# Attention with experts on one core: the first query job of a head behind the second score group, the last whole output tile behind the first group of last rows

## The chip, the core and the metric

The kernel runs on one core of one Trainium2 chip. The metric is the device time of one execution in microseconds (us), the median of several runs. A profile is one further execution, recorded instruction by instruction.

## The reference

Four sequences of 1024 tokens with 256 features are normalized, and from the normalized rows two things are made: a causal attention with 8 query heads of 128 that share one key and one value head, and a mixture of 8 experts of which each token uses two. The result is `x + attention * silu(experts)`.

```python
xn = _layernorm(x, axis=-1)
q = (xn @ Wq + bq)                  # 8 heads of 128
kv = xn @ Wkv + bkv                 # one key and one value head
q, k = q + pe, k + pe               # sinusoidal positions
scores = einsum('bhqd,bkd->bhqk', q, k) * scale
probs = softmax(where(causal, scores, finfo.min))
s = (probs @ v).reshape(B, T, 1024) @ Wo
g = silu(moe_top2(xn, router_w, router_b, w1, b1, w2, b2))
out = x + s * g
```

## The kernel before, in words

Three stages follow one another: `prologue` (normalize, route, split into halves), `experts`, and `attention` (L999 to L1520), which is the one that the change touches. Products are made in three passes of 16-bit halves (`PASSES`, L22): a value is kept as a high half and a low half, and high x high, high x low and low x high are added up.

**The attention stage.** There are 32 heads (4 sequences x 8 heads, `NH`), numbered n. The eight blocks of 128 query rows of a head are handled in five score groups i = 0 to 4, `GROUPS = ((7,), (6, 0), (5, 1), (4, 2), (3,))`: the block u needs u + 1 blocks of keys, so a group is 1024 columns of scores (the last one 512). A step is k = 5n + i. For every step, TensorE writes the scores of the group (`scores`, L1094); VectorE takes the row maxima (`maxima`, L1309); ScalarE the exponentials and their sums (`expo`, L1210); VectorE the reciprocals (L1340); ScalarE or GpSimd the high half of the probabilities (`high`, L1242 and L1435); VectorE, two steps later, the low half (`low`, L1345). The SP queue then issues transposes of the halves (`turn`, L1479), and in the following head TensorE multiplies them with the values, two blocks at a time in four value groups (`values`, L1124, in the order `PAIRS`). ScalarE and VectorE take high and low halves of that output (`o_high`, `o_low`).

**Jobs.** What a later head needs is projected in jobs, each into one PSUM bank of 128 x 512: two query jobs ("Q") per head, for the head after next, and in heads 4 to 7 of each of the first three sequences one key or value job ("K", "V") for the next sequence. Class `Jobs` (L290) lists them: `at` tells the step behind which a job is issued, `order` their order, `bank` the bank. Query jobs use bank "J" (`psJ`), key and value jobs bank "S" (`psS2`, the one of group 4's scores). A job is six matmuls of 512 columns (a value job 24 of 128) on TensorE (`project`, L1079), then VectorE adds the positions (`job_positions`, L1318; not for values), ScalarE takes the high half (`job_high`, L1229), VectorE the low half (`job_low`, L1326), which signals `jl_`. A job waits on `jl_` until the job before it in the same bank has been taken (`freed`, L1178-1179).

**Output tiles.** From head 9 on, TensorE also computes, at the end of each head, one whole tile of 128 output rows (`o_tile`, L1141, 24 matmuls of 256 columns) for the sequence before, into the same bank `psJ`. VectorE multiplies it by its gate at the start of the step after (`o_gated`, L1378, signals `ot_`), GpSimd adds the input rows, and the SP queue stores them. Because the bank is shared, the first query job of a head from 10 on waits for `ot_` (L1184-1185).

**The order around the change.** Every engine's order is written out by hand. TensorE's loop (L1170 to L1189) does for each head n and group i: the scores of the group; from i = 1 on value group i - 1 of the head before; the job of that step, if there is one; at i = 4, from head 9 on, an output tile. The first query job stands at i = 0, the key or value job at i = 1, the second query job at i = 2. ScalarE and VectorE take a job in the step after the one it was issued in. VectorE's order within a step is this (L1390 to L1405):

```python
if k - 1 in jobs.at:
    job_positions(jobs.at[k - 1])
if 1 <= k <= LAST:
    reciprocals(k - 1)
if k <= LAST and (k - 1) // 5 >= 1 and (k - 1) % 5:
    o_low((k - 1) // 5 - 1, (k - 1) % 5 - 1)
if k < LAST:
    maxima(k)
if k - 1 in jobs.at:
    job_low(jobs.at[k - 1])
if k >= 2:
    low(k - 2)
```

**The tail.** The last sequence's output is not done in tiles but as rows in four PSUM banks (`rows_out`, L1155), seven heads first and the eighth later. TensorE's tail (L1190 to L1206) is: the last whole output tile; a wait for the exponentials and for `al_`, the low output halves of head 30; last rows of pair 3 and of pair 0 for seven heads (42 matmuls each); then the value groups of head 31, in turn with the other rows.

Of the kernel before, what the change touches and what calls it, by code (L numbers as in the profile page):

```python
# [19 lines left out]
HEADS, HD = 8, 128  # L20
# [269 lines left out]
class Jobs:  # L290


    def __init__(self, heads):
        self.at, self.order, self.bank = {}, [], []
        for k in range(5 * heads):
            n, i = k // 5, k % 5
            b = n // HEADS
            job, bank = None, "J"
            if n == 0:
                job, bank = (("V", 0, 0), ("V", 0, 1), ("Q", 2, 0), ("Q", 2, 1), None)[i], ("J", "O0", "O1", "J", "")[i]  # L300
            elif i in (0, 2) and n + 2 < heads:
                job = ("Q", n + 2, i // 2)
            elif i == 1 and n % HEADS >= 4 and HEADS * (b + 1) < heads:
                job, bank = ("KKVV"[n % HEADS - 4], b + 1, n % 2), "S"
            if job:
                self.at[k] = len(self.order)
                self.order.append(job)
                self.bank.append(bank)

    def issued(self, k):  # L310

        return sum(1 for s in self.at if s < k)
# [686 lines left out]
def attention(nc, v):  # L999
# [6 lines left out]
    TILES = NT - QT  # L1006
    LAST = 5 * NH
    jobs = Jobs(NH)
# [3 lines left out]
    with ExitStack() as ctx:  # L1012
# [56 lines left out]
        def _(eng):  # L1069
# [24 lines left out]
            def scores(n, i):  # L1094

                k = 5 * n + i
# [10 lines left out]
                if i == 4 and k - 3 in jobs.at and jobs.bank[jobs.at[k - 3]] == "S":  # L1107
                    eng.wait_ge(jl_, jobs.at[k - 3] + 1)
# [15 lines left out]
            def values(n, s):  # L1124
# [14 lines left out]
                mm.then_inc(pv_, 1)  # L1139

# [29 lines left out]
            for n in range(NH):  # L1170
                for i in range(5):
                    k = 5 * n + i
                    scores(n, i)
                    if n and i:
                        values(n - 1, i - 1)
                    if k in jobs.at:
                        q = jobs.at[k]
                        if jobs.freed(q):  # L1178
                            eng.wait_ge(jl_, jobs.freed(q))
                        if jobs.bank[q] == "S":  # L1180
                            eng.wait_ge(ex_, 5 * n)
                        if n == 0:
                            eng.wait_ge(pl_, {"J": 4, "O0": 5, "O1": 6}[jobs.bank[q]])
                        if i == 0 and n >= HEADS + 2:  # L1184
                            eng.wait_ge(ot_, n - HEADS - 1)
                        project(*jobs.order[q], job_bank[jobs.bank[q]]).then_inc(jm_, 1)
                    if i == 4 and n > HEADS:
                        eng.wait_ge(jl_, jobs.issued(k + 1))
                        o_tile(n - HEADS - 1)  # L1189
            o_tile(TILES - 1)  # L1190
            eng.wait_ge(ex_, LAST - 1)
            eng.wait_ge(al_, 4 * (NH - 1))
            rows_out(3, 0, HEADS - 1)
            rows_out(0, 0, HEADS - 1)
# [14 lines left out]
        def _(eng):  # L1209
# [65 lines left out]
            for k in range(LAST + 2):  # L1275
                n, i = k // 5, k % 5
                if k - 1 in jobs.at:
                    job_high(jobs.at[k - 1])
# [19 lines left out]
        def _(eng):  # L1298
# [19 lines left out]
            def job_positions(q):  # L1318
                kind, m, j = jobs.order[q]
                if kind != "V":  # L1320
                    bank = job_bank[jobs.bank[q]]
                    eng.wait_ge(jm_, q + 1)
                    eng.scalar_tensor_tensor(bank, bank, SC / WS, pe_sb[:, j * 512:(j + 1) * 512],  # L1323
                                             ALU.mult, ALU.add).then_inc(jp_, 1)
# [65 lines left out]
            for k in range(LAST + 2):  # L1390
# [3 lines left out]
                if k - 1 in jobs.at:  # L1394
                    job_positions(jobs.at[k - 1])
# [6 lines left out]
                if k - 1 in jobs.at:  # L1402
                    job_low(jobs.at[k - 1])
# [144 lines left out]
```

## Time and profile before

| what | us |
|---|---|
| median of 3 runs | 1114.44 |
| the runs | 1115.57, 1114.44, 1110.93 |
| the profiled execution | 1122.9 |
| its span, first to last instruction | 1121.1 |
| mean granted clock of TensorE, of full speed | 0.989 |

The span holds 28441 instructions. The attention stage fills it from about 485 us on. Times in the rows further down are counted from the first instruction. In a timeline a row is one instruction, or several of one kind that follow one another (x6 are six): its start, its length, the engine, the line, what it writes and reads; in brackets the idle time ahead of it and who ended it. A matmul's end is a modelled one, and a following matmul normally starts before that end. The number of a head is worked out from the order of the query jobs.

### The profile page before, as it was taken

The numbers are of one execution on the slowest core, as the hardware profiler recorded it, in microseconds if no ns is written. First come the engines' busy times: TensorE is split into PE (matmuls) and PEld (weight loads), VectorE is DVE, ScalarE is ACT, GpSimd is POOL, SyncE is SP. The second block draws the span as 40 slices with busy tenths as digits, with TensorE's granted clock in tenths as the row PEclk, the third lists the DMA queues.
The fourth block names the chain that finished last, engine by engine and source line by source line (L and its number), as shares of the span: only waits on it lengthen the run. The fifth ranks groups of instructions, "written<-read, shape, count | busy, mean of one in ns | idle before, by whom it ended". The sixth has DMA issues, their size and how long they took to land.

```text
span 1121.1 us, 28441 instructions
## 1 busy us (share of the span) xinstructions
PE 1016.8 (91%) x10270; PEld 811.9 (72%) x10270; DVE 883.5 (79%) x1607; ACT 554.5 (49%) x1264; POOL 442.7 (39%) x499
## 2 busy tenths in 40 slices
PE   2536999999999999998989889999999999999997
PEld 1525888888888898755666667667777777777776
DVE  6894676676676454479999999998999999999972
ACT  3812223323323333346766666656666666666740
POOL 0013999899995100012323233333333333333331
PEclk9999999999999999998999999999999999999999
DMA  8547666756665512129987898988999888999993
GB/s 280 184 174 152 171 170 172 185 162 178 180 166 145 95 44 49 30 71 161 170 139 145 135 172 159 159 148 156 161 172 179 144 151 149 166 161 159 171 160 105
DMA packets 405896, 169.02 MB, mean 151 GB/s; under 512 B 348634, under 2 KB 396324, under 8 KB 405124
## 3 DMA queue, kind: packets, MB, share of 16 engines
q1 hardware_dynamic: 348704, 127.05, 57.0%
q10 hardware_dynamic: 50580, 22.45, 8.8%
q0 software_dynamic: 6480, 17.70, 7.4%
q8 instruction: 89, 1.46, 0.5%
q14 instruction: 43, 0.35, 0.1%
HBM read 51.66 MB, written 30.67 MB: 73 GB/s over the span
## 4 chain that ended last, share of the span: by engine, by line
DVE 27%; PE 20%; ACT 4%; issue 3%; DMA 2%; SPq 1%; ACTq 0%; DVEq 0%
DVE b_ph L1353 10%; DVE b_nmax L1314 8%; PE b_psO L1137 7%; PE b_psS L1118 5%; DVE b_outs L1361 2%; PE b_psJ L1075 2%; PE b_psJ L1151 2%; DVE b_psJ L1323 2%; ACT b_pr L1217 2%; PE b_psS L1162 2%; DMA b_pT<-b_ph 2%; ACT b_ph L1249 1%; PE b_psS L1075 1%; DVE b_Q L1337 1%; DVE b_f L1367 1%
## 5 line engine op out<-in xcount | busy, mean ns | idle before, releaser
L1442 POOL TENSOR_SCALAR b_ph<-b_pr,b_rrec 128x896 f16<-128x896 f32 (+4 forms) x160 | 109.3, 691 | 502.3 <-DVE b_rrec L1343 460.6
L938 ACT ACTIVATE h<-psU,bias 128x256 f32<-128x256 f32 (+1 forms) x320 | 125.1, 448 | 294.5 <-PE psU L858 170.4
L1217 ACT ACTIVATE b_pr<-b_psS,b_nmax 128x1024 f32<-128x1024 f32 (+7 forms) x256 | 187.3, 736 | 159.0 <-DVE b_nmax L1314 159.0
L1137 PE MATMUL b_psO<-b_pT,b_vp 128*128 128x128 f16 x3456 | 219.1, 221 | 20.5 <-DMA b_pT<-b_ph 20.4
L1137 PEld LDWEIGHTS b_psO<-b_pT,b_vp 128*128 128x128 f16 x3456 | 202.5, 99 | 29.6 <-issue 19.0
L858 PE MATMUL psU<-bxT,w_p 128*128 128x256 f16 (+1 forms) x1536 | 208.3, 273 | 16.5 <-DVE w_p L261 12.8
L1118 PE MATMUL b_psS<-b_kp,b_Q 128*128 128x512 f16 (+3 forms) x1152 | 220.2, 328 | 0.1
L1353 DVE SCALAR_TENSOR_TENSOR b_ph<-b_pr,b_rrec,b_ph 128x1024 f16<-128x1024 f32 (+7 forms) x256 | 209.9, 851 | 0.0
L871 PE MATMUL psY<-w_p,hp 128*128 x1512 | 206.4, 273 | 0.0
L959 DVE CAST hp<-h 128x512 f16<-128x512 f32 (+1 forms) x160 | 85.9, 537 | 137.1 <-ACT h L938 135.0
L1314 DVE TENSOR_REDUCE b_nmax<-b_psS 128x1 f32<-128x1024 f32 (+7 forms) x256 | 183.3, 748 | 8.6 <-PE b_psS L1121 8.6
L858 PEld LDWEIGHTS psU<-bxT,w_p 128*128 x1536 | 150.1, 99 | 35.6 <-issue 17.4
L1118 PEld LDWEIGHTS b_psS<-b_kp,b_Q 128*128 128x128 f16 x1152 | 103.6, 98 | 78.6 <-issue 2.3
L871 PEld LDWEIGHTS psY<-w_p,hp 128*128 128x128 f16 x1512 | 147.8, 98 | 17.4
L961 DVE TENSOR_TENSOR hp<-h,hp 128x512 f16<-128x512 f32 (+1 forms) x160 | 134.8, 843 | 5.5
L171 POOL DMA_INDIRECT rowx<-xn_split,who x71 | 80.4, 1132 | 106.7 <-DVE who L755 78.3
L1249 ACT ACTIVATE b_ph<-b_pr,b_rrec 128x1024 f16<-128x1024 f32 (+2 forms) x96 | 78.7, 853 | 0.5 <-DVE b_rrec L1343 0.5
L1451 POOL DMA_INDIRECT b_yg<-expert_outputs,pos x64 | 72.2, 1128 | 14.7 <-issue 14.1
L1361 DVE SCALAR_TENSOR_TENSOR b_outs<-b_psO,bias,b_outs 128x256 f16<-128x256 f32 x128 | 60.8, 475 | 19.0 <-ACT b_outs L1226 19.0
L1226 ACT ACTIVATE b_outs<-b_psO,bias 128x256 f16<-128x256 f32 x128 | 60.4, 472 | 19.0 <-PE b_psO L1137 19.0
L1151 PE MATMUL b_psJ<-b_wo,b_outs 128*128 128x256 f16 x576 | 66.8, 273 | 2.1 <-DVE b_G L1382 2.1
L250 POOL TENSOR_TENSOR w_p<-wstage,w_p 128x512 f16<-128x512 f32 x48 | 63.0, 1313 | 4.1
(184 smaller groups left out, 1138.8 us busy)
## 6 DMA issues: line engine op xcount, KB each, us to landing
wstage<-in_L_ffn_w SPq DMA_DIRECT2D x48, 256.0 KB
expert_rows<-rowx SPq DMA_DIRECT2D x67, 128.0 KB
expert_outputs<-y ACTq DMA_DIRECT2D x31, 256.0 KB, 3.3
a_x_all<-in_L_attn_x SPq DMA_DIRECT2D x8, 512.0 KB, 9.8
a_w_raw<-in_L_ffn_w SPq DMA_DIRECT2D x4, 1024.0 KB, 6.4
xn_split<-a_xp SPq DMA_DIRECT2D x4, 1024.0 KB, 5.0
b_pT<-b_ph SPq DMA_TRANSPOSE x256, 3.7
xn_turned<-a_xT SPq DMA_DIRECT2D x3, 1024.0 KB, 13.0
```

Source lines behind the costliest of these rows:

```text
L858: mm = eng.matmul(psU[w % U][:, g % 2, 0:tiles * P].rearrange("p (t r) -> p t r", t=tiles), weight(n, a * W1 + c * H + g * P, P), bxT[n % ...
L871: mm = eng.matmul(psY[n % 2][:, t, :], hp[n % 2][:, a, g, t * P:(t + 1) * P], weight(n, 2 * W1 + (2 * g + b) * D, D), start=(g == 0 and k ...
L938: a = eng.activation(h32[w % 4][:, g, 0:rows], psU[w % U][:, g, 0:rows], ACT.Relu, bias=bias[:, ds(e * HT + 2 * q + g, 1)], scale=1.0 / WS)
L961: eng.tensor_tensor(lo, full, hi, ALU.subtract).then_inc(hl_, 1)
L1118: mm = eng.matmul(dst, Q[n % 3][:, a, u * P:(u + 1) * P], kb[:, c, lo:lo + w], start=(kk == 0), stop=(kk == 2 and not last))
L1137: mm = eng.matmul(psO[w % 2][:, (u % 2) * P:(u % 2 + 1) * P], vb[:, a, j, :], pT[u][:, c * (u + 1) + j, :], start=(j == 0 and kk == 0), st ...
L1151: mm = eng.matmul(psJ[:, 0:D], outs[b % many][:, a, h, t * P:(t + 1) * P], wo_p[:, e, h, :], start=(h == 0 and kk == 0), stop=(h == HEADS ...
L1217: a = eng.activation(pr[k % 3][:, o:o + w], psS[BUF[i]][:, :, :].rearrange("p a n -> p (a n)")[:, o:o + w], ACT.Exp, bias=nmax[:, at:at + ...
L1249: a = eng.activation(ph[k % 4][:, 2 * o:2 * o + w], pr[k % 3][:, o:o + w], ACT.Copy, scale=rrec[:, at:at + 1])
L1314: a = eng.tensor_reduce(nmax[:, at:at + 1], psS[BUF[i]][:, :, :].rearrange("p a n -> p (a n)")[:, o:o + w], AX.X, ALU.max, negate=True)
L1353: a = eng.scalar_tensor_tensor(ph[k % 4][:, 2 * o + w:2 * o + 2 * w], pr[k % 3][:, o:o + w], rrec[:, at:at + 1], ph[k % 4][:, 2 * o:2 * o ...
L1442: a = eng.tensor_scalar(ph[k % 4][:, 2 * o:2 * o + w], pr[k % 3][:, o:o + w], rrec[:, at:at + 1], 1.0, ALU.mult, ALU.mult)
```

## The change

On TensorE the first query job of heads 1 to 29 moves from behind the scores of group 0 to behind those of group 1, ahead of the first value group; a key or value job, which stood behind that value group, now stands ahead of it too, right behind the first query job. The second query job stays behind value group 1. As several jobs can now belong to one step, `at` holds lists. The loops of ScalarE and VectorE go over these lists, so that both handle the first query job one step later than before. Head 0 keeps its order. The wait for `ot_` moves with the first query job. In the tail the last whole output tile moves from ahead of the last rows of pair 3 to behind them.

```diff
--- before.py
+++ after.py
@@ -295,21 +295,21 @@
         for k in range(5 * heads):
             n, i = k // 5, k % 5
             b = n // HEADS
-            job, bank = None, "J"
-            if n == 0:
-                job, bank = (("V", 0, 0), ("V", 0, 1), ("Q", 2, 0), ("Q", 2, 1), None)[i], ("J", "O0", "O1", "J", "")[i]
-            elif i in (0, 2) and n + 2 < heads:
-                job = ("Q", n + 2, i // 2)
-            elif i == 1 and n % HEADS >= 4 and HEADS * (b + 1) < heads:
-                job, bank = ("KKVV"[n % HEADS - 4], b + 1, n % 2), "S"
-            if job:
-                self.at[k] = len(self.order)
-                self.order.append(job)
-                self.bank.append(bank)
+            if n == 0 and i < 4:
+                self.add(k, (("V", 0, 0), ("V", 0, 1), ("Q", 2, 0), ("Q", 2, 1))[i], ("J", "O0", "O1", "J")[i])
+            elif n and i in (1, 2) and n + 2 < heads:
+                self.add(k, ("Q", n + 2, i - 1), "J")
+            if i == 1 and n % HEADS >= 4 and HEADS * (b + 1) < heads:
+                self.add(k, ("KKVV"[n % HEADS - 4], b + 1, n % 2), "S")
+
+    def add(self, k, job, bank):
+        self.at.setdefault(k, []).append(len(self.order))
+        self.order.append(job)
+        self.bank.append(bank)
 
     def issued(self, k):
 
-        return sum(1 for s in self.at if s < k)
+        return sum(len(q) for s, q in self.at.items() if s < k)
 
     def turned(self, q):
 
@@ -1104,8 +1104,9 @@
                     eng.wait_ge(jl_, jobs.count("Q", n))
                 if i == 0 and n and n % HEADS == 0:
                     eng.wait_ge(jl_, jobs.count("K", n // HEADS))
-                if i == 4 and k - 3 in jobs.at and jobs.bank[jobs.at[k - 3]] == "S":
-                    eng.wait_ge(jl_, jobs.at[k - 3] + 1)
+                for q in jobs.at.get(k - 3, ()):
+                    if i == 4 and jobs.bank[q] == "S":
+                        eng.wait_ge(jl_, q + 1)
                 kb = kp[n // HEADS % many]
                 for u in GROUPS[i]:
                     o = GROUP_OF[u][1]
@@ -1138,6 +1139,19 @@
                                             start=(j == 0 and kk == 0), stop=(j == u and kk == 2))
                 mm.then_inc(pv_, 1)
 
+            def work(q, k):
+
+                n, bank = k // 5, jobs.bank[q]
+                if jobs.freed(q):
+                    eng.wait_ge(jl_, jobs.freed(q))
+                if bank == "S":
+                    eng.wait_ge(ex_, 5 * n)
+                if n == 0:
+                    eng.wait_ge(pl_, {"J": 4, "O0": 5, "O1": 6}[bank])
+                if k % 5 == 1 and bank == "J" and n >= HEADS + 2:
+                    eng.wait_ge(ot_, n - HEADS - 1)
+                project(*jobs.order[q], job_bank[bank]).then_inc(jm_, 1)
+
             def o_tile(c):
 
                 t, b = c % QT, c // QT
@@ -1171,26 +1185,21 @@
                 for i in range(5):
                     k = 5 * n + i
                     scores(n, i)
+                    if n and i == 1:
+                        for q in jobs.at.get(k, ()):
+                            work(q, k)
                     if n and i:
                         values(n - 1, i - 1)
-                    if k in jobs.at:
-                        q = jobs.at[k]
-                        if jobs.freed(q):
-                            eng.wait_ge(jl_, jobs.freed(q))
-                        if jobs.bank[q] == "S":
-                            eng.wait_ge(ex_, 5 * n)
-                        if n == 0:
-                            eng.wait_ge(pl_, {"J": 4, "O0": 5, "O1": 6}[jobs.bank[q]])
-                        if i == 0 and n >= HEADS + 2:
-                            eng.wait_ge(ot_, n - HEADS - 1)
-                        project(*jobs.order[q], job_bank[jobs.bank[q]]).then_inc(jm_, 1)
+                    if n == 0 or i != 1:
+                        for q in jobs.at.get(k, ()):
+                            work(q, k)
                     if i == 4 and n > HEADS:
                         eng.wait_ge(jl_, jobs.issued(k + 1))
                         o_tile(n - HEADS - 1)
-            o_tile(TILES - 1)
             eng.wait_ge(ex_, LAST - 1)
             eng.wait_ge(al_, 4 * (NH - 1))
             rows_out(3, 0, HEADS - 1)
+            o_tile(TILES - 1)
             rows_out(0, 0, HEADS - 1)
             values(NH - 1, 0)
             values(NH - 1, 1)
@@ -1274,8 +1283,8 @@
                                bias=bias[:, col:col + 1]).then_inc(pa_, 1)
             for k in range(LAST + 2):
                 n, i = k // 5, k % 5
-                if k - 1 in jobs.at:
-                    job_high(jobs.at[k - 1])
+                for q in jobs.at.get(k - 1, ()):
+                    job_high(q)
                 if 1 <= k <= LAST and (k - 1) % 5 in BY_ACT:
                     high(k - 1)
                 if k < LAST:
@@ -1391,16 +1400,16 @@
                 n, i = k // 5, k % 5
                 if i == 0 and n >= HEADS + 2:
                     o_gated(n - HEADS - 2)
-                if k - 1 in jobs.at:
-                    job_positions(jobs.at[k - 1])
+                for q in jobs.at.get(k - 1, ()):
+                    job_positions(q)
                 if 1 <= k <= LAST:
                     reciprocals(k - 1)
                 if k <= LAST and (k - 1) // 5 >= 1 and (k - 1) % 5:
                     o_low((k - 1) // 5 - 1, (k - 1) % 5 - 1)
                 if k < LAST:
                     maxima(k)
-                if k - 1 in jobs.at:
-                    job_low(jobs.at[k - 1])
+                for q in jobs.at.get(k - 1, ()):
+                    job_low(q)
                 if k >= 2:
                     low(k - 2)
                 if k < LAST and n:
```

## Rows read from the trace of the kernel before

**Rows 1.** The page, its first part: busy time, share of the span, instructions.
```profile
PE 1016.8 (91%) x10270; PEld 811.9 (72%) x10270; DVE 883.5 (79%) x1607; ACT 554.5 (49%) x1264; POOL 442.7 (39%) x499
```

**Rows 2.** Busy time by stretch: length, then each engine, granted clock, DMA share, GB/s.
```profile
640.00:660.00 20.00, 15.89 (x176) 11.62 (x177) 19.23 (x37) 13.12 (x30) 6.38 (x7) 1.00 1.09 162
...
800.00:820.00 20.00, 19.65 (x210) 14.58 (x209) 19.20 (x35) 13.67 (x32) 7.48 (x9) 1.00 1.08 175
```

**Rows 3.** Timeline of TensorE, a head without key or value job.
```profile
791.33 1.46 PE L1075 MATMUL b_psJ<-xTb_next,wq_late 128*128 128x512 f16 x6 [0.47 <-issue]
...
797.91 0.22 PE L1121 MATMUL b_psS<-maskb,idb 128*128 128x128 bf16 x1
797.96 0.67 PE L1137 MATMUL b_psO<-b_pT,b_vp 128*128 128x128 f16 x9
798.47 1.46 PE L1075 MATMUL b_psJ<-xTb_next,wq_late 128*128 128x512 f16 x6
...
808.81 0.22 PE L1121 MATMUL b_psS<-maskb,idb 128*128 128x128 bf16 x1
809.37 1.46 PE L1075 MATMUL b_psJ<-xTb_next,wq_late 128*128 128x512 f16 x6 [0.34 <-issue]
```

**Rows 4.** Timeline of VectorE, the same head.
```profile
795.91 0.74 DVE L1337 SCALAR_TENSOR_TENSOR b_Q<-b_psJ,bias,b_Q 128x512 f16<-128x512 f32 x1
...
797.88 0.17 DVE L1343 RECIPROCAL b_rrec<-b_rsum 128x2 f32<-128x2 f32 x1 [0.57 <-ACT b_pr L1217]
798.24 0.48 DVE L1361 SCALAR_TENSOR_TENSOR b_outs<-b_psO,bias,b_outs 128x256 f16<-128x256 f32 x1 [0.20 <-ACT b_outs L1226]
...
808.85 0.42 DVE L1382 SCALAR_TENSOR_TENSOR b_G<-b_psJ,b_G 128x256 f32<-128x256 f32 x1
```

**Rows 5.** Waits from 520 us on: waiter, awaited, us in total, times, longest.
```profile
PE b_psJ L1075 <- issue: 7.7, 18, 0.8
...
DVE b_psS L1323 <- PE b_psS L1075: 5.3, 5, 2.0
```

**Rows 6.** Timelines of both engines around group 2 of head 12.
```profile
721.12 0.22 PE L1121 MATMUL b_psS<-maskb,idb 128*128 128x128 bf16 x1
...
721.38 1.29 DVE L1314 TENSOR_REDUCE b_nmax<-b_psS 128x1 f32<-128x768 f32 x2 [0.27 <-PE b_psS L1121]
722.59 0.74 DVE L1337 SCALAR_TENSOR_TENSOR b_kp<-b_psS,bias,b_kp 128x512 f16<-128x512 f32 x1
```

**Rows 7.** Timelines of both engines, head 1: a query job waits for its bank.
```profile
507.07 0.75 DVE L1337 SCALAR_TENSOR_TENSOR b_Q<-b_psJ,bias,b_Q 128x512 f16<-128x512 f32 x1
...
507.88 2.74 PE L1075 MATMUL b_psJ<-xTb_next,wq_late 128*128 128x512 f16 x6 [3.44 <-DVE b_Q L1337]
```

**Rows 8.** Timeline of VectorE: maxima of group 0 in heads 2 and 3.
```profile
528.18 1.21 DVE L1314 TENSOR_REDUCE b_nmax<-b_psS 128x1 f32<-128x1024 f32 x1
...
545.76 1.21 DVE L1314 TENSOR_REDUCE b_nmax<-b_psS 128x1 f32<-128x1024 f32 x1
```

**Rows 9.** Timeline of TensorE, head 12: a value group waits for transposed weights.
```profile
715.96 2.67 PE L1137 MATMUL b_psO<-b_pT,b_vp 128*128 128x128 f16 x45 [1.16 <-DMA b_pT<-b_ph]
```

**Rows 10.** Timelines of both engines in the tail.
```profile
1084.21 0.47 DVE L1361 SCALAR_TENSOR_TENSOR b_outs<-b_psO,bias,b_outs 128x256 f16<-128x256 f32 x1
...
1084.37 2.78 PE L1151 MATMUL b_psJ<-b_wo,b_outs 128*128 128x256 f16 x24 [2.06 <-DVE b_G L1382]
```

**Rows 11.** Timeline of TensorE: two value groups of 45 matmuls behind a wait.
```profile
564.51 4.30 PE L1137 MATMUL b_psO<-b_pT,b_vp 128*128 128x128 f16 x45 [1.99 <-DMA b_pT<-b_ph]
...
640.38 2.67 PE L1137 MATMUL b_psO<-b_pT,b_vp 128*128 128x128 f16 x45 [1.78 <-DMA b_pT<-b_ph]
```

## The prediction, before the change was measured

> **What bounds the kernel now.** The page first: TensorE is counted busy for 91% of the span [rows 1]. That share mixes stages, so the next view is the busy time in stretches of 20 us of the attention stage [rows 2]. Between 640 and 660 us (heads without an output tile) VectorE is busy 19.2 of 20 us and TensorE 15.9; between 800 and 820 us (heads that end with an output tile) both are nearly full, VectorE 19.2 and TensorE 19.7. So in the later heads neither engine has room, and the order of the waits between them decides. For that, read one head in order of time on both engines.
>
> TensorE's timeline [rows 3]: a head without a key or value job lasts 809.37 - 791.33 = 18.04 us from first query job to first query job. TensorE loses time at one place, ahead of that job: the mask matmul of score group 0 ends at 809.03 and the job starts at 809.37. The view calls it "issue"; the code shows a wait for ot_ (L1184-1185), and VectorE's row settles it: the gating that signals ot_ ends at 808.85 + 0.42 = 809.27 [rows 4]. The idle time counted is 0.34 us; as a matmul without a wait starts about 0.16 us before the visible end of the one ahead (797.96 against 797.91 + 0.22) [rows 3], the time lost is 0.50. Over the kernel there are 18 such waits, 7.7 us idle [rows 5], so 7.7 + 18 x 0.16 = 10.6 us lost.
>
> VectorE's timeline [rows 4]: it waits twice per head for ScalarE, 0.57 us for the sums of group 1 and 0.20 us for an output half. Its own work is therefore 18.04 - 0.77 = 17.3 us. The row to keep in mind is the low half of the first query job at 795.91: it ends at 796.65, and the second query job, which needs the same bank (L1178-1179), starts at 798.47. The bank was given back 1.8 us early.
>
> **The change, part by part.** No instruction is added or removed; the order changes on TensorE, ScalarE and VectorE, the latter two because their loops follow the group behind which a job is issued. No transfer's place in the SP or POOL queue changes.
>
> *(a) First query job behind group 1 on TensorE.* The wait for ot_ now comes some 1.4 us of scores later, past 809.27, and is covered. This gives back at most the 10.6 us, and I take all.
>
> *(b) The low half behind the maxima of group 2 on VectorE.* This is the term that decides. VectorE's loop does, in step k: positions of the job of step k-1, reciprocals, output half, maxima of k, low half of the job of step k-1 (L1394-1403). A first query job at step 5n+1 therefore gets its low half behind the maxima of step 5n+2. The second job is issued at step 5n+2 as before, behind the scores of group 2 and nine value matmuls, and still waits for that low half. So TensorE must now see group 2 finished, VectorE must take its maxima, then do the low half, and only then does the bank come free. Let e be the visible end of group 2's scores, 797.91 + 0.22 = 798.13 [rows 3]. Maxima start 0.04 later (721.12 + 0.22 to 721.38), and the following instruction starts 1.21 later (722.59) [rows 6]. The low half takes 0.75, and TensorE starts 0.06 after its end, read at the one place where it already waits for it (507.07 + 0.75, 507.88) [rows 7]. The second job starts at e + 0.04 + 1.21 + 0.75 + 0.06 = e + 2.06; before it started at 798.47 = e + 0.34. The stall is 1.72 us, counted as about 1.55 us idle. It follows from the order in the program, and in these heads TensorE has nothing to hide it: its work in a plain head is 18.04 - 0.50 = 17.54, so the head becomes 17.54 + 1.72 = 19.3 us. VectorE's 17.3 us fit into that, so it does not become the bound. Everything behind the second job (groups 3 and 4, three value groups, the output tile, the next head) is queued behind this wait, and VectorE's later maxima wait with it. Heads 9 to 29 end with an output tile and have both jobs: 21 x 1.72 = 36.1 us. Bounds: if VectorE arrives at group 2 late by both of its present waits, 1.72 + 0.77 = 2.5 us (52 us in all); if the pipelines overlap more than the rows show, by the 0.50 us that a wait costs today, 1.2 us (25 us). I take 1.72, which is built from rows of the same operations.
>
> *(c) The key or value job ahead of the first value group, in twelve heads.* On TensorE it is a swap of equal work. On VectorE its positions come ahead of the reciprocals and fill the 0.57 us wait, and five waits for that job, 5.3 us in all [rows 5], shrink. Where TensorE is the bound this changes nothing; in heads 4 to 7 it may save.
>
> *(d) Heads 1 to 8, without output tiles.* One lasts 545.76 - 528.18 = 17.58 us, at VectorE's pace [rows 8]; TensorE's work there is 17.54 less an output tile, so the stall falls into time in which it would wait anyway. VectorE loses its 0.77 us of waits at best and gains a short wait for group 3, as the second job is later. Bounds: -0.77 and, by the 0.50 us of a wait today, +0.5 per head, -6 and +4 in all. I take -2, for the waits of (c).
>
> *(e) Transposes.* A value group that waited 1.16 us for its transposed weights in head 12 [rows 9] now starts later. I take -1.
>
> *(f) The tail.* Before, the last whole output tile starts at 1084.37, behind the gating of the tile before it. After, the first group of last rows is ahead of it, and that waits for al_ (L1192), the low output half that ends at 1084.21 + 0.47 = 1084.68 [rows 10]. TensorE idles on until then and the rest is equal work: +0.4 us. The idle time is not filled, since the work put there needs something that ends later still.
>
> Sum: -10.6 + 36.1 - 2 - 1 + 0.4 = +22.9 us. The profiled execution takes 1122.9 us with a span of 1121.1; the median of the runs, 1114.44, is 0.8% less. The sum is 2.04% of the one and 2.06% of the other, so it is added to the median: 1114.44 + 22.9 = 1137.3, and I say 1137.
>
> **One rule of the skill.** The view by stretches shows a granted clock of 1.00 through 800 to 820 us [rows 2], the level of 2.4 GHz, although TensorE waits in each of these heads. After a wait of 1.78 us, 45 value matmuls took 2.67 us; after one of 1.99 they took 4.30 [rows 11], and after 2.06 in the tail an output tile ran at its usual 2.78 [rows 10]. A counted idle of 1.55 lies on the undisturbed side. The Trainium skill, TensorE: Matmul & The Clock Gate, section "A second HAM failure mode: psum-queue depth-cycling", says that micro-idles between matmul groups, repeated often as banks are cycled, can make the clock swing between its levels; by it the stall would be paid again in slow matmuls, and the trace's 1.00 with a shorter wait per head does not bear it out so far.
>
> **The rivals.**
> 1. *The clock falls behind the stall.* For it: 1.55 is not far from the 1.99 us after which it did. Against: the 1.78 and 2.06 rows. Price: 4.30 - 2.67 = 1.63 us in each of 21 heads, 34 us more, 1171 us. Chance 0.09.
> 2. *Faster: the wait for ot_ was the price and the bank comes back in time.* The place is the second query job. If VectorE reached the low half before group 2's scores were done, the stall would be nothing and the 10.6 us of (a) and 3 of (d) and (e) remained: about 1101 us. It decides where the stall is under 10.6 / 21 = 0.5 us per head. The Trainium skill, Perfetto Trace Analysis, section "Optimization Strategy", tells to find the gaps on the bound engine and let what they wait for come sooner, which is the case for this change. Against it stands the order in VectorE's loop: maxima of group 2 alone take 1.21 us and cannot start before e. Chance 0.04.
> 3. *A draw.* The stall costs nearer 0.6 us, because TensorE gets ahead elsewhere and VectorE, not TensorE, sets the pace after the change. For it: VectorE's 19.2 of 20 busy. Against: 17.3 us of work in a head of 19.3. About 21 x 0.6 - 10.6 - 3 = -1: 1113 us. Chance 0.07.
>
> **How the numbers follow.** The forecast has 0.80: with the stall between 1.2 and 2.5 us it gives 1126 to 1154, and with the early heads' bounds a few us more. The range of 1122 to 1155 leaves out rivals 1 to 3 and a little of the forecast. About 0.5% is what a measurement of this kernel tells from no change. Slower by more: 0.80 + 0.09 = 0.89; within: 0.07; faster: 0.04.
>
> **What the changed profile would show.** Right: no idle time ahead of the first query job, and ahead of the second one an idle time of about 1.5 us in each of heads 9 to 29, released by VectorE's low half; a plain head of 19.3 us and one with a key or value job some 1.3 us longer; VectorE waiting for group 2's last matmul in each head; heads 2 and 3 still near 17.6 us; the last whole tile behind 42 matmuls of last rows, with the wait ahead of those ending about 0.4 us later. Wrong: a second job without idle time ahead of it, or the 1.00 of the granted clock below 0.95 in the stretches from 680 us on (rival 1).

## The result and the profile after

The changed kernel takes 1138.22 us, median of 5 runs (1136.58 to 1144.44). The ratio to the kernel before is 1.0216, with a 95% interval of 1.0185 to 1.0247. The prediction said 1137, in a range of 1122 to 1155. The profiled execution took 1144.44 us with a span of 1142.6. That is 21.5 us more than the profiled execution before; the medians lie 23.8 apart. Both profiled executions lie above their medians, by 8.5 us before and 6.2 after.

The page's first part shows the same instructions and nearly the same busy times as [rows 1], in a longer span:

```profile
PE 1017.3 (89%) x10270; PEld 809.5 (71%) x10270; DVE 883.5 (77%) x1607; ACT 559.9 (49%) x1264; POOL 453.1 (40%) x499
```

So the time was not added as work, and the next view is the busy time by stretch. Two rows cover the steady part of the attention stage, first of the kernel before, then of the changed one (columns as in [rows 2]):

```profile
680.00:1080.00 400.00, 388.13 (x4167) 291.26 (x4165) 375.69 (x693) 260.28 (x589) 137.59 (x172) 1.00 0.94 160
```

```profile
680.00:1080.00 400.00, 368.62 (x3936) 276.36 (x3934) 360.29 (x660) 250.49 (x560) 137.55 (x164) 1.00 0.82 152
```

TensorE was idle for 11.9 of these 400 us and is idle for 31.4 now, at a granted clock of 1.00 in both. The view of waits from 520 us on (columns as in [rows 5]) names the wait:

```profile
PE b_psJ L1075 <- DVE b_Q L1346: 42.0, 28, 2.3
...
DVE b_nmax L1323 <- PE b_psS L1122: 22.1, 60, 1.6
...
PE b_psO L1138 <- DMA b_pT<-b_ph: 6.7, 8, 1.6
```

The wait called "issue" ahead of a query job [rows 5] has no line among them any more. In its place TensorE waits 42 us for VectorE's half of a query job. The timeline of TensorE through one plain head shows where; the rows answer to [rows 3]:

```profile
797.10 1.46 PE L1075 MATMUL b_psJ<-xTb_next,wq_late 128*128 128x512 f16 x6
...
802.26 0.22 PE L1122 MATMUL b_psS<-maskb,idb 128*128 128x128 bf16 x1
802.32 0.67 PE L1138 MATMUL b_psO<-b_pT,b_vp 128*128 128x128 f16 x9
804.53 1.47 PE L1075 MATMUL b_psJ<-xTb_next,wq_late 128*128 128x512 f16 x6 [1.54 <-DVE b_Q L1346]
...
816.35 1.46 PE L1075 MATMUL b_psJ<-xTb_next,wq_late 128*128 128x512 f16 x6
```

The first query job runs without idle time ahead of it. The second one waits 1.54 us. In each of heads 10 to 29 the timeline has the same 1.54 at this place (2.26 in head 9): 20 x 1.54 = 30.8 us, nearly all of the 31.4 us of idle time in the stretch. The head lasts 816.35 - 797.10 = 19.25 us, where it was 18.04. VectorE's timeline of the same head answers to [rows 4] and shows what TensorE waits for:

```profile
801.25 0.17 DVE L1352 RECIPROCAL b_rrec<-b_rsum 128x2 f32<-128x2 f32 x1 [0.25 <-ACT b_pr L1226]
801.61 0.48 DVE L1370 SCALAR_TENSOR_TENSOR b_outs<-b_psO,bias,b_outs 128x256 f16<-128x256 f32 x1 [0.20 <-ACT b_outs L1235]
802.52 1.29 DVE L1323 TENSOR_REDUCE b_nmax<-b_psS 128x1 f32<-128x768 f32 x2 [0.42 <-PE b_psS L1122]
803.73 0.74 DVE L1346 SCALAR_TENSOR_TENSOR b_Q<-b_psJ,bias,b_Q 128x512 f16<-128x512 f32 x1
...
815.13 1.23 DVE L1323 TENSOR_REDUCE b_nmax<-b_psS 128x1 f32<-128x1024 f32 x1 [0.40 <-PE b_psS L1122]
```

Read the two together. Group 2's scores end at 802.26 + 0.22 = 802.48. VectorE has waited 0.42 us for them; it takes their maxima from 802.52, then the low half from 803.73 to 804.47, and at 804.53 the second job starts. It is the chain that term (b) wrote down.

By the start of the maxima of group 0, head by head, the 21.5 us of the span divide so: ahead of head 0's, +0.5; heads 0 to 8, -2.6 (163.47 to 160.89); heads 9 to 29, +21.1 (394.78 to 415.91); head 30, nothing; from head 31 to the end, +2.5 (52.98 to 55.48). The tail's part shows on TensorE's timeline, where 42 matmuls of last rows now stand ahead of the last whole tile [rows 10]:

```profile
1089.54 2.67 PE L1138 MATMUL b_psO<-b_pT,b_vp 128*128 128x128 f16 x45 [1.64 <-DMA b_pT<-b_ph]
...
1104.25 6.41 PE L1176 MATMUL b_psS<-b_wo,b_outs 128*128 128x256 f16 x42 [2.36 <-DVE b_outs L1370]
1110.49 2.78 PE L1165 MATMUL b_psJ<-b_wo,b_outs 128*128 128x256 f16 x24
1113.12 4.75 PE L1176 MATMUL b_psS<-b_wo,b_outs 128*128 128x256 f16 x42
```

### The profile page after: what moved, and what is told of

It is laid out like the page before. It is cut to its first block, busy times and chain, and to the rows that moved or that the text cites. A ratio compares the mean times of both kernels' runs of the same rounds, so it can differ in the third digit from the quotient of the medians.

```text
span 1142.6 us, 28441 instructions
## 1 busy us (share of the span) xinstructions
PE 1017.3 (89%) x10270; PEld 809.5 (71%) x10270; DVE 883.5 (77%) x1607; ACT 559.9 (49%) x1264; POOL 453.1 (40%) x499
## 4 chain that ended last, share of the span: by engine, by line
PE 38%; DVE 16%; ACT 2%; DMA 1%; issue 1%; SPq 0%; ACTq 0%; DVEq 0%
PE b_psS L1119 12%; PE b_psO L1138 11%; DVE b_nmax L1323 7%; PE b_psJ L1075 6%; PE b_psJ L1165 5%; DVE b_ph L1362 4%; DVE b_Q L1346 2%; PE b_psS L1176 2%; PE b_psS L1075 1%; DVE b_outs L1370 1%; ACT b_pr L1226 1%; PE b_psS L1122 1%; DMA b_pT<-b_ph 1%; ACT b_outs L1235 0%; SPq L1495 0%
## 5 line engine op out<-in xcount | busy, mean ns | idle before, releaser
L1451 POOL TENSOR_SCALAR b_ph<-b_pr,b_rrec 128x896 f16<-128x896 f32 (+4 forms) x160 | 125.3, 792 | 514.0 <-DVE b_rrec L1352 462.4
L1138 PE MATMUL b_psO<-b_pT,b_vp 128*128 128x128 f16 x3456 | 214.5, 219 | 8.8 <-DMA b_pT<-b_ph 8.5
L1119 PE MATMUL b_psS<-b_kp,b_Q 128*128 128x512 f16 (+3 forms) x1152 | 217.1, 328 | 1.5 <-ACT b_pr L1226 1.4
L1138 PEld LDWEIGHTS b_psO<-b_pT,b_vp 128*128 128x128 f16 x3456 | 199.1, 98 | 22.9 <-issue 9.0
L1362 DVE SCALAR_TENSOR_TENSOR b_ph<-b_pr,b_rrec,b_ph 128x1024 f16<-128x1024 f32 (+7 forms) x256 | 207.6, 841 | 0.0
L959 DVE CAST hp<-h 128x512 f16<-128x512 f32 (+1 forms) x160 | 89.7, 560 | 141.4 <-ACT h L938 140.8
L961 DVE TENSOR_TENSOR hp<-h,hp 128x512 f16<-128x512 f32 (+1 forms) x160 | 127.5, 797 | 5.6
L1460 POOL DMA_INDIRECT b_yg<-expert_outputs,pos x64 | 69.4, 1085 | 14.6 <-issue 13.4
L1075 PE MATMUL b_psJ<-b_xTb_other,wq_late 128*128 128x512 f16 x192 | 48.3, 389 | 24.4 <-DVE b_Q L1346 24.4
```

The source lines that it names most:

```text
L961: eng.tensor_tensor(lo, full, hi, ALU.subtract).then_inc(hl_, 1)
L1075: mm = eng.matmul(out, lhs(a, c), rhs(b, c), start=(k == 0), stop=(k == 3 * DC - 1))
L1119: mm = eng.matmul(dst, Q[n % 3][:, a, u * P:(u + 1) * P], kb[:, c, lo:lo + w], start=(kk == 0), stop=(kk == 2 and not last))
L1138: mm = eng.matmul(psO[w % 2][:, (u % 2) * P:(u % 2 + 1) * P], vb[:, a, j, :], pT[u][:, c * (u + 1) + j, :], start=(j == 0 and kk == 0), st ...
L1362: a = eng.scalar_tensor_tensor(ph[k % 4][:, 2 * o + w:2 * o + 2 * w], pr[k % 3][:, o:o + w], rrec[:, at:at + 1], ph[k % 4][:, 2 * o:2 * o ...
L1451: a = eng.tensor_scalar(ph[k % 4][:, 2 * o:2 * o + w], pr[k % 3][:, o:o + w], rrec[:, at:at + 1], 1.0, ALU.mult, ALU.mult)
```

## The experiments

All ratios are to runs of the kernel before on the same chip. The first four runs ask whether VectorE's order makes the stall, the next two try the other parts of the change alone, and the last two ask what the new order is worth without its stall.

**1. The low half ahead of the maxima.** The changed kernel, except that VectorE does its half of the first query job ahead of the maxima of group 2. TensorE's order is untouched.

```diff
+                mine = list(jobs.at.get(k - 1, ()))
+                if n and i == 2 and mine:
+                    job_low(mine.pop(0))
                 if k < LAST:
                     maxima(k)
-                for q in jobs.at.get(k - 1, ()):
+                for q in mine:
                     job_low(q)
```

> The changed kernel, with one step moved on VectorE alone: the low half of a head's first query job ahead of the maxima of group 2 instead of behind them. TensorE's order stays that of the changed kernel. My theory (TensorE waits at the second query job for that low half): the low half can now start as soon as ScalarE has its high half, which follows an output half and a weighting, about 0.2 us behind the end of group 2's scores instead of 1.25 us; the wait ahead of the second job falls from 1.54 us idle to about 0.5, the maxima are later instead, and a plain head goes from 19.25 to about 18.4 us: some 0.8 us in each of 21 heads, 1121 us (1116 to 1128). Rival A (the loss lies in TensorE's new order itself, the two score groups back to back and the job ahead of the value group): TensorE's order is the same, so 1138 us, within 4.

Measured: 1123.21 us (1118.55 to 1134.96), ratio 1.0109 (1.0038 to 1.0179). A plain head lasts 18.35 us. The timelines of both engines:

```profile
809.94 0.75 DVE L1346 SCALAR_TENSOR_TENSOR b_Q<-b_psJ,bias,b_Q 128x512 f16<-128x512 f32 x1 [0.49 <-ACT b_Q L1248]
810.61 1.28 DVE L1323 TENSOR_REDUCE b_nmax<-b_psS 128x1 f32<-128x768 f32 x2
```

```profile
810.75 1.47 PE L1075 MATMUL b_psJ<-xTb_next,wq_late 128*128 128x512 f16 x6 [0.64 <-DVE b_Q L1346]
```

The same job in the same place on TensorE costs 0.9 us less per head once VectorE's order is turned round, so the maxima in front of the low half were most of the stall. What is left has another cause: the low half itself waits 0.49 us for ScalarE, which does the high half (b_Q of L1248).

**2. Both halves early.** Also, ScalarE does its half right behind the exponentials of group 1 instead of one step later, and VectorE's half comes right behind the reciprocals.

```diff
                 if k < LAST:
                     expo(k)
+                    if n and i == 1 and k in jobs.at:
+                        job_high(jobs.at[k][0])
...
                 if 1 <= k <= LAST:
                     reciprocals(k - 1)
+                mine = list(jobs.at.get(k - 1, ()))
+                if n and i == 2 and mine:
+                    job_low(mine.pop(0))
```

> The changed kernel, with the first query job taken earlier on both engines: ScalarE takes its high half right behind the exponentials of group 1, VectorE its low half right behind the reciprocals of group 1, ahead of the output half and of the maxima of group 2. TensorE's order stays that of the changed kernel. My theory: the bank comes back before the scores of group 2 end, there is no idle time ahead of the second query job, VectorE is the bound again with some 0.75 us of waits per head, a plain head takes about 18.0 us: 1114 us (1109 to 1119), all of the loss undone though TensorE's order is the changed one. Rival A: 1138 us, within 4.

Measured: 1106.5 us (1104.83 to 1112.54), ratio 0.9923 (0.9894 to 0.9951): faster than the kernel before. Heads 9 to 29 take 385.31 us (394.78 in the profiled execution of the kernel before, 390.82 in that of experiment 5, where these heads have the same order), a plain one 17.98. The timelines of both engines:

```profile
807.54 0.17 DVE L1357 RECIPROCAL b_rrec<-b_rsum 128x2 f32<-128x2 f32 x1 [0.25 <-ACT b_pr L1226]
808.12 0.75 DVE L1351 SCALAR_TENSOR_TENSOR b_Q<-b_psJ,bias,b_Q 128x512 f16<-128x512 f32 x1 [0.41 <-ACT b_Q L1248]
...
809.18 1.28 DVE L1328 TENSOR_REDUCE b_nmax<-b_psS 128x1 f32<-128x768 f32 x2
```

```profile
808.93 1.47 PE L1075 MATMUL b_psJ<-xTb_next,wq_late 128*128 128x512 f16 x6 [0.26 <-DVE b_Q L1351]
```

The low half now ends at 808.87, ahead of the maxima, and 0.26 us of the 1.54 are left. The move on TensorE is thus not a loss in itself. The expected time missed by 7.5 us. Six of the eight heads with a key or value job take 18.81 to 18.87 us, some 0.67 less than the 19.5 before; with the other two (19.01 and 19.45) that is 4.6 us that had not been counted. The rest was not traced.

**3. The low half still later.** The opposite of experiment 1: VectorE's half of the first query job, and its part of a key or value job, also behind the low half of group 0's probabilities.

```diff
-                for q in jobs.at.get(k - 1, ()):
-                    job_low(q)
+                if not (n and i == 2):
+                    for q in jobs.at.get(k - 1, ()):
+                        job_low(q)
                 if k >= 2:
                     low(k - 2)
+                if n and i == 2:
+                    for q in jobs.at.get(k - 1, ()):
+                        job_low(q)
```

> The changed kernel, with the suspected wait made longer: VectorE takes the low half of the first query job behind the low half of group 0's probabilities (1.20 us), which follows the maxima of group 2. My theory: TensorE idles 2.74 us instead of 1.54 ahead of each second query job, 21 x 1.2 = 25 us more, and some in the heads before, 1165 us (1160 to 1171) if its clock holds; if a wait of that length lets the clock fall, the matmuls behind it cost up to 1.6 us more per head, and it is up to 1199 us with a granted clock below 1 in all stretches. Rival A: the wait does not bound, under 1145 us.

Measured: 1190.49 us (1188.83 to 1193.03), ratio 1.0684 (1.0652 to 1.0716), between the two sums. A plain head in which the clock held lasts 20.45 us, which is 19.25 plus the 1.20 us by which the idle time grew (1.54 to 2.74): what stands ahead of the low half goes into the head in full. More came from the clock. Behind 9 of the 24 waits of 2.73 or 2.74 us the granted clock of the next 9 us was 0.81 to 0.83, behind the other 15 it was 1.00. In eight of the nine the six matmuls of the job took longer than 1.47 us (1.66 to 2.74); in the ninth (head 14, the second row) the scores of group 3 behind them did, 1.75 us where 0.98 is usual. Rows of TensorE's timeline:

```profile
574.16 2.74 PE L1075 MATMUL b_psJ<-xTb_next,wq_late 128*128 128x512 f16 x6 [2.74 <-DVE b_Q L1346]
...
788.84 1.75 PE L1119 MATMUL b_psS<-b_kp,b_Q 128*128 128x512 f16 x6
...
831.43 1.47 PE L1075 MATMUL b_psJ<-xTb_next,wq_late 128*128 128x512 f16 x6 [2.74 <-DVE b_Q L1346]
832.73 0.98 PE L1119 MATMUL b_psS<-b_kp,b_Q 128*128 128x512 f16 x6
```

In heads 9 to 29 the growth is 35.1 us, of which 21 x 1.20 = 25.2 is the longer wait; six heads with a key or value job in which the clock fell, 23.4 us long where the two in which it held take 21.8, make most of the other 10. Heads 1 to 8 grew by 17.3 us, which was not taken apart; the granted clock was 0.91 in most of their stretches.

**4. The second job in another bank.** In heads without a key or value job the second query job goes to the bank of score group 4, so that it doesn't need the bank of the first. Group 4's scores wait for its low half.

```diff
-                self.add(k, ("Q", n + 2, i - 1), "J")
+                self.add(k, ("Q", n + 2, i - 1), "S" if i == 2 and (n % HEADS < 4 or HEADS * (b + 1) >= heads) else "J")
...
-                for q in jobs.at.get(k - 3, ()):
+                for q in [p for s in (k - 4, k - 3, k - 2) for p in jobs.at.get(s, ())]:
```

> The changed kernel, with the second query job in another PSUM bank, that of group 4's scores, in the heads that have no key or value job (13 of heads 9 to 29); group 4's scores then wait for its low half. No engine's order changes. My theory: there the second job no longer waits for the first one's low half, the idle time ahead of it is gone, group 4's scores may wait 0.3 us, VectorE bounds again at 17.3 us and 0.5 of waits, so a plain head takes about 17.8 us, shorter than the 18.04 before the change; heads with a key or value job keep their wait of 1.54 us and 20.6 us: 13 x 1.45 = 19 us less, 1119 us (1114 to 1124). Rival A: 1138 us, within 4, as the order is the same. Rival B (VectorE's and ScalarE's new order bounds, whatever the bank): 1138 us too, with VectorE full.

Measured: 1138.35 us (1137.84 to 1138.68), ratio 1.0214 (1.0188 to 1.024). The expectation missed: nothing is gained. The timelines of TensorE and VectorE say why:

```profile
817.44 1.46 PE L1075 MATMUL b_psS<-xTb_next,wq_late 128*128 128x512 f16 x6
...
823.73 0.81 PE L1119 MATMUL b_psS<-b_kp,b_Q 128*128 128x512 f16 x3 [1.57 <-DVE b_Q L1346]
```

```profile
817.14 1.29 DVE L1323 TENSOR_REDUCE b_nmax<-b_psS 128x1 f32<-128x768 f32 x2 [0.36 <-PE b_psS L1122]
...
821.65 1.27 DVE L1323 TENSOR_REDUCE b_nmax<-b_psS 128x1 f32<-128x640 f32 x2
822.84 0.74 DVE L1346 SCALAR_TENSOR_TENSOR b_Q<-b_psS,bias,b_Q 128x512 f16<-128x512 f32 x1
```

The second job has no wait any more, but group 4's scores have one of 1.57 us, again for a low half behind maxima, this time those of group 3. VectorE takes 6.44 us from the maxima of group 2 to the end of that low half without a pause, TensorE 12.64 from the scores behind it to the end of the next group 2; with 0.19 us between the engines that is 19.27, by chance nearly the 19.25 of the changed kernel. The Trainium skill, Perfetto Trace Analysis, section "Matmuls", says that independent groups of matmuls should rotate through banks, so that emptying one overlaps the matmuls of the next. Here another bank alone moved the wait from one bank to the next. What took most of it away was the other order on the engines that empty the banks (experiment 2).

**5. The tail's part alone.** The kernel before, with the last whole tile behind the first group of last rows.

```diff
-            o_tile(TILES - 1)
             eng.wait_ge(ex_, LAST - 1)
             eng.wait_ge(al_, 4 * (NH - 1))
             rows_out(3, 0, HEADS - 1)
+            o_tile(TILES - 1)
```

> The kernel before, with the change of the tail alone. My theory: TensorE idles in the tail until the low output half of head 30 instead of until the gating of the tile before, about 0.4 us longer, so 1115 us, not told apart from no change (within 3 us of the kernel before); in the trace the wait ahead of the last rows is 2.4 us where it was 2.06, and the matmuls behind it keep 4.75 us for 42. Rival C (the tail is part of the loss): over 1119 us.

Measured: 1114.94 us, 10 runs, ratio 1.0001 (0.9973 to 1.0029). TensorE's timeline:

```profile
1079.74 6.41 PE L1162 MATMUL b_psS<-b_wo,b_outs 128*128 128x256 f16 x42 [2.36 <-DVE b_outs L1361]
```

The wait is 2.36 us, where it was 2.06 [rows 10]. In this profiled run, as in that of the changed kernel, 42 matmuls behind it took 6.41 us instead of the expected 4.75. In experiments 1 and 3 the same wait was followed by the usual 4.75. So the tail is worth between 0.3 and 2 us in one execution, less than the runs can tell.

**6. The key or value job alone.** The kernel before, with only the key or value job ahead of the first value group; the first query job stays behind group 0.

```diff
-            elif i in (0, 2) and n + 2 < heads:
-                job = ("Q", n + 2, i // 2)
-            elif i == 1 and n % HEADS >= 4 and HEADS * (b + 1) < heads:
-                job, bank = ("KKVV"[n % HEADS - 4], b + 1, n % 2), "S"
...
+            elif n and i in (0, 2) and n + 2 < heads:
+                self.add(k, ("Q", n + 2, i // 2), "J")
+            if i == 1 and n % HEADS >= 4 and HEADS * (b + 1) < heads:
+                self.add(k, ("KKVV"[n % HEADS - 4], b + 1, n % 2), "S")
...
+                    if n and i == 1:
+                        for q in jobs.at.get(k, ()):
+                            work(q, k)
                     if n and i:
                         values(n - 1, i - 1)
```

> The kernel before, with one part of the change alone: the key or value job of twelve heads ahead of the first value group. The first query job stays behind group 0, the tail is as before. My theory: TensorE's work is the same, VectorE no longer waits up to 2 us for the job, heads 12 to 15 and 20 to 23 go from 19.52 to about 18.9 us, 5 us less, and one or two more in heads 4 to 7: 1108 us (1105 to 1112); so the whole loss lies with the first query job, and this part pays. Rival A in its other form (two jobs, or a job ahead of the value group, hold up TensorE): over 1116 us.

Measured: 1112.42 us, 10 runs, ratio 0.9983 (0.9955 to 1.001). The expected gain is not there: heads 12 to 15 and 20 to 23 still take 19.50 to 19.58 us, and heads 4 to 7 take what they take in experiment 5, within 0.2. TensorE's timeline of one such head:

```profile
745.02 1.46 PE L1075 MATMUL b_psJ<-xTb_next,wq_late 128*128 128x512 f16 x6 [0.53 <-issue]
...
753.50 1.46 PE L1075 MATMUL b_psJ<-xTb_next,wq_late 128*128 128x512 f16 x6
```

The gap ahead of the first query job is as before, the second has none: TensorE, with that gap, sets the pace, and moving equal work about on it bought nothing. So neither of the parts tried alone makes the 24 us; what is left is the first query job, with VectorE's half of it.

**7. Both halves early, and the tail without its wait.** Experiment 2, and in the tail the last rows start with the six heads whose output is ready.

```diff
             eng.wait_ge(ex_, LAST - 1)
+            eng.wait_ge(al_, 4 * (NH - 2))
+            rows_out(3, 0, HEADS - 2)
             eng.wait_ge(al_, 4 * (NH - 1))
-            rows_out(3, 0, HEADS - 1)
+            rows_out(3, HEADS - 2, HEADS - 1)
             o_tile(TILES - 1)
```

> The kernel of the second experiment (both halves of the first query job taken early), with the last rows of pair 3 split in the tail: six heads' rows first, which wait only for the output halves of head 29, then the seventh, then the last whole tile. My theory: TensorE no longer idles for 1.1 to 2.4 us at the start of the tail, 1.5 us less than 1106.5: 1105 us (1102 to 1108), faster than the kernel before by 0.8 to 1.0%. Rival: the transposes of the last head end later than the rows, TensorE waits for them instead, and it is 1106.5.

Measured: 1102.67 us (1100.87 to 1105.2), ratio 0.9895 (0.9858 to 0.9933). TensorE's timeline has no idle time ahead of the last rows:

```profile
1061.12 2.78 PE L1165 MATMUL b_psJ<-b_wo,b_outs 128*128 128x256 f16 x24
1063.74 4.75 PE L1176 MATMUL b_psS<-b_wo,b_outs 128*128 128x256 f16 x42
```

From head 31's first maxima to the end it takes 51.4 us, against 54.7 in experiment 2. Of these 3.3 us 1.14 are the wait that went; another 1.9 are waits of head 31 for transposed weights, which were 2.95 us in experiment 2 and 1.05 here. The intervals of the two ratios overlap, so the runs alone don't tell this version from experiment 2. It has the lowest median of the study.

**8. VectorE's last wait filled.** Experiment 7, with `whole_f` put where VectorE waits 0.41 us for the high half, and `weigh` on ScalarE one step earlier to feed it.

```diff
-                    if i == 1:
+                    if i == 0:
                         weigh(seq[n - 1])
...
+                if k < LAST and n and i == 2:
+                    whole_f(seq[n - 1])
                 if n and i == 2 and mine:
                     job_low(mine.pop(0))
...
-                    if i == 2:
-                        whole_f(seq[n - 1])
```

> The kernel of the seventh experiment, with VectorE's wait ahead of the early low half (0.41 us per head) filled: the second expert's weighting (0.40 us of VectorE work, which stood behind the low half of group 0) is done there, and ScalarE's first weighting, on which it rests, one step earlier, where ScalarE waits 2.8 us. My theory: in heads 9 to 29 VectorE and TensorE are both near their work now (17.3 and 17.5 us of 17.98), so a plain head falls to 17.6 to 17.8 us; heads 1 to 8 and the rest gain up to 0.4 each: 6 to 9 us less than 1102.7, 1095 us (1092 to 1100). Rival: TensorE, which waits 0.26 us for its bank, is the bound and the gain stays under 2 us, 1101 to 1104.

Measured: 1103.94 us (1095.53 to 1110.81, 9 runs), ratio 0.9899 (0.9863 to 0.9935): no gain over experiment 7 that can be told. Some plain heads do last 17.6 us, but others 17.9 to 19.1, with another wait on TensorE's timeline:

```profile
817.33 1.47 PE L1075 MATMUL b_psJ<-xTb_next,wq_late 128*128 128x512 f16 x6
...
824.17 0.84 PE L1138 MATMUL b_psO<-b_pT,b_vp 128*128 128x128 f16 x12 [0.91 <-DMA b_pT<-b_ph]
```

The second job has no wait left here, and a value group waits for transposed weights instead. In heads 9 to 29 these waits come to 6.5 us in 8 places, against 2.7 in one place in experiment 7. One profiled execution of each is compared here, and such waits vary from one execution to the next (3.8 us in 3 places in the kernel before, 3.0 in one in experiment 5). What makes these transfers late was not tried.

## Why the prediction was right

*(a) The wait for ot_* is gone, as said: from head 9 on no idle time stands ahead of a first query job.

*(b) The stall* is right in place, size and releaser: 1.54 us counted where 1.55 was said, 19.25 us per plain head where 19.3 was said, 20.54 to 20.59 with a key or value job where some 1.3 more than a plain one was said. Experiments 1 and 3 show that it follows what stands ahead of the low half on VectorE, in both directions, and experiment 2 that nearly nothing is left of it when that half comes early.

*(c) and (d) The key or value job, and heads 1 to 8:* -2.6 us between the two profiled executions, where -2 was said. That this fits is chance. Heads 0 to 8 took 163.5, 160.8 and 161.8 us in the three traces with the old place of the first query job (the kernel before, experiments 5 and 6) and 160.9 in the changed kernel, so a term of 2 us is not told from their spread. In heads 12 to 15 and 20 to 23, where TensorE is the bound, the key or value job's new place changes nothing, and in heads 4 to 7 not more than 0.2 us each (experiment 6); heads 2 and 3 stay near 17.6. Two things in these heads were not worked out. In head 8, in which the granted clock was 0.91 (640 to 660 us), 1.7 us were lost. And the wait of 3.44 us ahead of head 1's first query job [rows 7] went with the change, as the job now comes later; the six matmuls behind it take 1.47 us instead of 2.74:

```profile
508.37 1.47 PE L1075 MATMUL b_psJ<-xTb_next,wq_late 128*128 128x512 f16 x6 [0.48 <-DVE b_Q L1346]
```

*(e) The transposes* were read from a row that does not come back. Heads 9 to 29 became 21.1 us longer between the two profiled executions, where 36.1 less 10.6 and 1 is 24.5. Experiments 5 and 6 are further traces of the old place of the first query job, and in them the same heads take 390.82 and 390.87 us instead of 394.78. Head 12, which waited 1.16 us for transposed weights [rows 9] and took 20.84 us, has no such wait there and takes 19.52 and 19.58. The start of the maxima of group 0 in heads 9 and 30, from VectorE's timeline of experiment 5:

```profile
652.47 1.21 DVE L1314 TENSOR_REDUCE b_nmax<-b_psS 128x1 f32<-128x1024 f32 x1
...
1043.29 1.21 DVE L1314 TENSOR_REDUCE b_nmax<-b_psS 128x1 f32<-128x1024 f32 x1
```

So some 4 us of the 394.78 belong to that one execution, and not to the kernel's order. From 390.82 to 415.91 the growth is 25.1 us, and (a) and (b) alone had said 36.1 - 10.6 = 25.5. A plain head grew by 1.21 us, which is 1.72 less the 0.50 that the wait for ot_ had cost. The heads with a key or value job grew by 1.03 to 1.08, as the wait that went was longer there (0.47 to 0.53 us idle, and 0.16 more each). Head 9 grew by 2.2; its wait was 2.26 us, and the granted clock around it 0.91.

*(f) The tail* took 2.5 us more in this pair of traces, where 0.4 was said. The wait for the output half itself is right: 2.36 us instead of 2.06, +0.3. Two things came on top in this execution: 6.41 - 4.75 = 1.66 us of slower matmuls behind the wait, and 0.6 us ahead of it, where head 31's wait for transposed weights grew from 0.47 to 1.64 us. The row taken for the clock, "after 2.06 in the tail an output tile ran at its usual 2.78", did not carry to 2.36. But a pair of traces can't size this term: from head 31's first maxima to the end the old tail took 53.0 and 56.6 us (the kernel before, experiment 6), the changed one 53.4 to 58.4 in six traces (the changed kernel, experiments 1 to 5).

What carries the forecast is (a) and (b), 25.5 us where 25.1 were measured. The small terms, -2.6 us in sum, are less than what two profiled executions of one order differ by, so how close 1137 came to 1138.2 is in part luck.

*The rivals.* Rival 1, the clock: through 680 to 1080 us it stayed at 1.00, and each of the 20 second jobs of heads 10 to 29, behind a wait of 1.54 us, took its usual 1.47. It was 0.91 in the stretches ahead (640 to 680 us, heads 8 and 9) and again in the tail (1100 to 1120 us, behind the wait of 2.36), which are not the stall of 1.54; the sign named for this rival, below 0.95 from 680 us on, covers the tail's stretch all the same. The Trainium skill's rule on repeated micro-idles (TensorE: Matmul & The Clock Gate, section "A second HAM failure mode: psum-queue depth-cycling") is not borne out by these 20 waits; experiment 3, with 2.74 us at the same place, shows a lower clock behind 9 of 24 waits. Rival 2, faster, needed the bank back in time, and VectorE's order excludes it; with that order changed it is what experiment 2 measured, 1106.5 where the rival gave 1101. Rival 3, a draw, needed VectorE to set the pace; in the changed kernel it waits for group 2's scores in every such head.

## What to carry to other kernels

When a job moves one step later on the engine that issues it, look up where the engine that empties its buffer has that work in its own order: here a wait of 0.34 us went and one of 1.54 us came, because the emptying slipped behind maxima that could not start yet. Another buffer did not help while the order of the emptying engine stayed (experiment 4); taking the emptying early on both engines that share it turned the same move from 2.2% slower into 0.8% faster, and 1.05% with the tail mended, a difference between the last two that the runs don't tell apart.

## What was not expected of the hardware

Equal waits did not cost equal clock. Behind a wait of 2.36 us at the same place of the program, 42 matmuls took 6.41 us in two profiled runs (the changed kernel, experiment 5) and 4.75 in two others (experiments 1 and 3). Behind 2.73 or 2.74 us the granted clock of the next 9 us was 0.81 to 0.83 in 9 of 24 cases and 1.00 in 15 (experiment 3). All nine lie in the twelve heads with a key or value job, none in the twelve plain heads; that is one trace, and why it is so was not found. Nor does the length of the wait alone set the order: 3.31 us in head 1 of experiment 3 were followed by six matmuls in their usual 1.47 us, and 0.75 us in head 8 of the changed kernel, shortly behind a wait of 1.44, by six in 2.74. At 1.54 us, in heads 10 to 29 of the changed kernel, the clock never fell.
